# Weight preparation for the second half's stages, moved from the setup into the second to fourth samples of lane 0

## What is computed

```python
x = x + tanh(g_xattn[i]) * xattn_i(layernorm(x), ctx)
x = x + tanh(g_ffn[i])   * ffn_i(layernorm(x))          # i = 0..3
# ffn_0: two linear maps with quantised inputs and weights, depthwise convolution and silu between them
# ffn_1: a router picks one of 8 experts for each token
# ffn_2: rmsnorm, causal self attention, rmsnorm, gated silu map of width 1024 (up, down)
# ffn_3: three blocks of quantised linear maps with low-rank parts, layernorm and gelu
```

## Time and profile before

| | us |
|---|---|
| median of the runs | 2938.9 (2935.18 to 2942.4) |
| the profiled execution | 2956.94 |
| its span (first to last instruction) | 2955.7 |
| PE busy in it | 2666.5 (90%) |
| PE's weight loads | 2164.5 (73%) |
| DVE busy | 2224.2 (75%) |
| ACT busy | 1743.2 (59%) |
| POOL busy | 980.4 (33%) |
| granted TensorE clock, mean | 0.967 of full |

### The profile page before, as it was taken

The page is one execution under the profiler, slowest core; times in us unless marked ns, Lnnn a source line. Parts: engine busy times, 40 slices in busy tenths (PEclk is TensorE's granted clock), DMA queues, the critical chain, the costliest instruction groups (busy, mean ns, idle before and its releaser), DMA issues.

```text
span 2955.7 us, 61780 instructions
## 1 busy us (share of the span) xinstructions
PE 2666.5 (90%) x24164; PEld 2164.5 (73%) x24164; DVE 2224.2 (75%) x5402; ACT 1743.2 (59%) x4657; POOL 980.4 (33%) x1404
## 2 busy tenths in 40 slices
PE   6888999898899989898899999899999998997988
PEld 4767777677677767677677777778777877776766
DVE  7677686868676776867677777778877886867888
ACT  4667667676566666676465555556565655653433
POOL 2222313222433433223533442333322333224545
PEclk8899999999999999999999999999999999998999
DMA  5000000000011211100011221000000001001010
GB/s 179 5 21 11 21 10 19 10 14 17 19 46 51 69 46 37 31 12 26 19 39 57 62 73 35 24 23 17 21 17 16 20 18 30 5 5 33 29 40 19
DMA packets 84091, 92.20 MB, mean 31 GB/s; under 512 B 15252, under 2 KB 77208, under 8 KB 83800
## 3 DMA queue, kind: packets, MB, share of 16 engines
q1 hardware_dynamic: 75352, 59.91, 6.5%
q0 software_dynamic: 8448, 28.34, 3.3%
HBM read 65.36 MB, written 22.85 MB: 30 GB/s over the span
## 4 chain that ended last, share of the span: by engine, by line
PE 53%; DVE 32%; ACT 6%; issue 4%; POOL 3%; DMA 1%; another core or an unknown queue 1%; SPq 0%; DVEq 0%; POOLq 0%; ACTq 0%
PE psum L387 12%; PE psum L363 11%; PE psum L356 9%; PE psum L413 5%; DVE tiny L735 5%; DVE big L743 4%; PE psum L425 3%; PE psum L542 3%; PE psum L380 2%; PE psum L370 2%; PE psum L377 2%; DVE big L822 2%; PE psum L536 2%; DVE xn L716 1%; DVE psum L732 1%
## 5 line engine op out<-in xcount | busy, mean ns | idle before, releaser
L387 PE MATMUL psum<-ident,big 128*128 128x128 f32 x2816 | 423.6, 286 | 75.9 <-ACT big L1221 36.3
L1399 POOL TENSOR_TENSOR tiny<-tiny,minus_half 128x1 f32<-128x1 f32 x224 | 129.7, 579 | 994.8 <-DVE tiny L706 993.9
L1221 ACT ACTIVATE big<-big 128x512 f32<-128x512 f32 x512 | 312.3, 632 | 227.8 <-DVE big L743 226.1
L387 PEld LDWEIGHTS psum<-ident,big 128*128 128x128 f32 x2816 | 324.1, 145 | 145.4 <-ACT big L1221 68.7
L735 DVE TENSOR_REDUCE tiny<-psum 128x8 f32<-128x1024 f32 x256 | 312.8, 1222 | 54.3 <-PE psum L413 49.4
L743 DVE TENSOR_TENSOR big<-psum,tiny 128x512 f32<-128x512 f32 x512 | 330.0, 686 | 8.8
L413 PE MATMUL psum<-head_keys,small 64*128 64x256 f32 x2048 | 284.1, 400 | 23.6 <-ACT big L1228 13.9
L1414 POOL TENSOR_TENSOR head_keys<-big,head_rows 128x512 f32<-128x512 f32 x256 | 265.4, 1056 | 0.0
L413 PEld LDWEIGHTS psum<-head_keys,small 64*128 64x128 f32 x2048 | 183.7, 187 | 77.0 <-issue 56.4
L1439 POOL TENSOR_TENSOR big<-big,tiny 128x512 f32<-128x512 f32 x128 | 137.1, 1073 | 307.9 <-DVE tiny L778 307.5
L1265 ACT ACTIVATE big<-psum,tiny 128x128 f32<-128x128 f32 x512 | 182.1, 384 | 40.2 <-DVE tiny L773 39.9
(11 more groups left out here) (319 smaller groups left out, 6656.3 us busy)
## 6 DMA issues: line engine op xcount, KB each, us to landing
ctxT<-in_ctxT SPq DMA_DIRECT2D x64, 128.0 KB
after_L_xattn<-x SPq DMA_DIRECT2D x64, 128.0 KB, 1.7
mixture_out<-spare SPq DMA_DIRECT2D x46, 128.0 KB
x_in<-in_x SPq DMA_DIRECT2D x32, 128.0 KB
mixture_in<-xn SPq DMA_DIRECT2D x32, 128.0 KB, 1.7
x_in<-after_L_xattn SPq DMA_DIRECT2D x32, 128.0 KB
bx_in<-after_L_xattn SPq DMA_DIRECT2D x32, 128.0 KB, 2.1
out<-bout SPq DMA_DIRECT2D x32, 128.0 KB, 1.7
```

The source lines that it names most:

```text
L387: last = pe.transpose(bank[:, k * P:(k + 1) * P], src[:, k * P:(k + 1) * P], identity)
L1221: last = act.activation(flat, flat, ACT.Exp, scale=DH ** -0.5)
```

## The change

The setup ends after the fold of L1 and the planning constants. The fold of L2, the scalings for ffn_2 and the fold of L3 become turns of lane 0, at the start of the bit stage of its second, third and fourth sample. There the folds use lane 0's own bank b, free at that point. Lane 0's first wait on PE is now for the fold of L1. The second half waits for the moved steps under new names.

```diff
 SETUP = {
-    "pe": "o_L0 mean o_L1 o_L2 o_L3",
-    "dve": "ident fold_L0 bias_L0 abs clip deq r1 r2 r3 w1 s1 s2 w2 fold_L1 bias_L1 plan "
-           "fold_L2 bias_L2 down norms fold_L3 bias_L3",
+    "pe": "o_L0 mean o_L1",
+    "dve": "ident fold_L0 bias_L0 abs clip deq r1 r2 r3 w1 s1 s2 w2 fold_L1 bias_L1 plan",
...
+LATE_AT = {(1, "bit"): "L2", (2, "bit"): "self", (3, "bit"): "L3"}
...
 def pe_lane(pe, m, t):
     if t.n == 0:
-        pe.wait_ge(*m.s.dve.at(0, "setup.bias_L3"))
+        pe.wait_ge(*m.s.dve.at(0, "setup.bias_L1"))
...
         if p == 0:
-            pe.wait_ge(*m.s.dve.at(0, "setup.norms"))
+            pe.wait_ge(*m.late.dve.at(0, "late.down"))
...
+def pe_late(pe, m, t, p, l):
+    if t.n or LATE_AT.get((p, l)) not in ("L2", "L3"):
+        return
+    of = LATE_AT[(p, l)]
+    pe.wait_ge(m.loads[of], m.loaded[of])
+    pe.wait_ge(*t.dve.at(p + FREE[l][0], FREE[l][1]))
+    pe.wait_ge(*m.late.dve.at(0, f"late.fold_{of}"))
+    pe_fold(pe, m, of, t.b).then_inc(*m.late.pe.tell(0, f"late.o_{of}"))
+    yield
...
+def dve_late(dve, m, t, p, l):
+
+    if t.n or (p, l) not in LATE_AT:
+        return
+    of, w = LATE_AT[(p, l)], m.w
+    if of == "self":
+        for name, n in (("selfq", 0), ("selfk", 0), ("selfv", 0), ("gate", 1), ("up", 1)):
+            for k in range(KD):
+                last = dve.tensor_scalar(w[name][:, k, :], w[name][:, k, :], m.norms[:, n, k:k + 1], None, ALU.mult)
+        last.then_inc(*m.late.dve.tell(0, "late.norms"))
+        yield
+        dve.tensor_scalar(w["down"][:], w["down"][:], m.gf["L2"], 0.5, ALU.mult, ALU.mult
+                          ).then_inc(*m.late.dve.tell(0, "late.down"))
+        yield
+        return
+    dve_fold(dve, m, of).then_inc(*m.late.dve.tell(0, f"late.fold_{of}"))
+    yield
+    dve.wait_ge(*m.late.pe.at(0, f"late.o_{of}"))
+    dve.tensor_copy(m.out_bias[of][:], t.b[:, 0:D]).then_inc(*m.late.dve.tell(0, f"late.bias_{of}"))
+    yield
```

`pe_bitlinear` and `dve_bitlinear` call these first. The waits of PE, POOL and DVE for the old names move to the new ones. The order strings of all engines, those of the last part too, are written anew; their beginnings on PE:

```diff
-        "1323232314121333222111332321321213123241142222111133332211222112133122133213134223012301201031200213"
+        "1213114323231211222333112123132323131232401011103303322223311333113221300302321002213023103010323001"
```

More of the change, by code:

```diff
@@ L113 @@
 }
+LATE = {"pe": "o_L2 o_L3", "dve": "fold_L2 bias_L2 norms down fold_L3 bias_L3", "act": "", "pool": ""}
 LORA = {"pe": " ".join(f"m{n}" for n in range(NL)),
@@ L548, in pe_bitlinear @@
 def pe_bitlinear(pe, m, t, p, l):
+    yield from pe_late(pe, m, t, p, l)
     yield from pe_plan(pe, m, t, p, l)
@@ L637, in pe_fold @@
             pe.matmul(bank[:, 0:D], m.bvb[:, k, :], m.w[l + "o"][:, k, :], start=k == 0, stop=False)
-    pe.matmul(bank[:, 0:D], m.ones[0:1, :], m.w[l + "bo"][:], start=l == "L1", stop=True
-              ).then_inc(*m.s.pe.tell(0, f"setup.o_{l}"))
+    return pe.matmul(bank[:, 0:D], m.ones[0:1, :], m.w[l + "bo"][:], start=l == "L1", stop=True)
 def pe_constants(pe, m):
@@ L646, in pe_constants @@
     yield
-    for l in ("L1", "L2", "L3"):
-        pe.wait_ge(m.loads[l], m.loaded[l])
-        pe_fold(pe, m, l, m.setup_bank)
-        yield
+    pe.wait_ge(m.loads["L1"], m.loaded["L1"])
+    pe.wait_ge(*m.s.dve.at(0, "setup.fold_L1"))
+    pe_fold(pe, m, "L1", m.setup_bank).then_inc(*m.s.pe.tell(0, "setup.o_L1"))
+    yield
 def pe_lora(pe, m):
@@ L795, in then @@
         dve.wait_ge(*t.dve.at(p, f"{l}.{name}"))
+    yield from dve_late(dve, m, t, p, l)
     yield from dve_plan(dve, m, t, p, l)
@@ L1033, in dve_fold @@
             last = dve.tensor_copy(m.bvb[:, k, :], w[l + "bv"][:, k:k + 1].to_broadcast([P, P]))
-    last.then_inc(*m.s.dve.tell(0, f"setup.fold_{l}"))
+    return last
 def dve_bias(dve, m, l):
@@ L1068, in dve_constants @@
         yield
-    dve_fold(dve, m, "L1")
+    dve_fold(dve, m, "L1").then_inc(*m.s.dve.tell(0, "setup.fold_L1"))
     yield
@@ L1080, in dve_constants @@
     last.then_inc(*m.s.dve.tell(0, "setup.plan"))
-    yield
-    dve_fold(dve, m, "L2")
-    yield
-    dve_bias(dve, m, "L2")
-    dve.tensor_scalar(w["down"][:], w["down"][:], m.gf["L2"], 0.5, ALU.mult, ALU.mult
-                      ).then_inc(*m.s.dve.tell(0, "setup.down"))
-    yield
-    for name, n in (("selfq", 0), ("selfk", 0), ("selfv", 0), ("gate", 1), ("up", 1)):
-        for k in range(KD):
-            last = dve.tensor_scalar(w[name][:, k, :], w[name][:, k, :], m.norms[:, n, k:k + 1], None, ALU.mult)
-    last.then_inc(*m.s.dve.tell(0, "setup.norms"))
-    yield
-    dve_fold(dve, m, "L3")
-    yield
-    dve_bias(dve, m, "L3")
     yield
@@ L1144, in vector_program @@
     dve.wait_ge(*m.s.act.at(0, "setup.tanh"))
-    dve_fold(dve, m, "L0")
+    dve_fold(dve, m, "L0").then_inc(*m.s.dve.tell(0, "setup.fold_L0"))
     dve_bias(dve, m, "L0")
@@ L1151, in vector_program @@
         dve.wait_ge(t.ystored, 16 * 2 * tiles_of(t.n))
-    dve.wait_ge(*m.s.dve.at(0, "setup.bias_L3"))
+    dve.wait_ge(*m.late.dve.at(0, "late.bias_L3"))
     dve_lora(dve, m)
@@ L1521, in pool_lane @@
         if p == 0:
-            pool.wait_ge(*m.s.dve.at(0, "setup.bias_L2"))
+            pool.wait_ge(*m.late.dve.at(0, "late.bias_L2"))
         yield from pool_cross(pool, m, t, p, "L2", t.x[:])
@@ L1731, in shared_memory @@
         keep_signals(m.s, e, Signals(sem(e + "_setup"), names))
+    m.late = Lane()
+    for e in ("pe", "dve"):
+        keep_signals(m.late, e, Signals(sem(e + "_late"), [(0, f"late.{n}") for n in LATE[e].split()]))
     groups = ("L0", "L0 ffn", "L1", "router", "L2", "L3")
```

219 lines of the change are left out of this document (110 added, 109 removed).

## The result

The kernel after the change took 2899.9 us (median of four runs, 2898.3 to 2901.0), against 2937.0 us before (the three runs of above and a fourth, 2933.1 to 2942.4). The ratio is 0.9872 [0.9856, 0.9888]: 37 us less, where the prediction said 8 less and no more than 23. The profiled execution of after took 2899.15 us, which is its median; that of before took 2956.94 us, 20 us above its own median. So the two profiles differ by 58 us, of which only 37 are in the medians, and where sizes matter they are taken from runs with the kernel before beside them.

A forecast was written before the change was run, and what follows sets the result against it. PE was taken to set the pace most of the time, DVE in stretches. Terms -11.4 + 0 + 3.5 + 2.4 + 0.6 - 3.0 summed to -7.9 us, 2931 us as a median, range 2916 to 2950.

The forecast's parts named there:

- The early start: 55.3 to 115.7 us: lane 0 starts 60.4 us sooner, moving one L0 stage into idle PE time; -11.4 us.
- the better mix behind: Behind the early stretch: lane 0's bit stage starts sooner, spreading the crowd at 160 to 180 us; -3.0 us.
- PE would be busy for over 50 us in the stretch: Sign that the forecast is right: PE busy above 50 us from 55.3 to 115.7 us.
- The folds: First half, on PE: the two moved folds return as turns where PE is near its limit; +3.5 us.
- the 7.4 us on DVE coming back: Lane 0's later bit stages: DVE has the moved work there, charged at its 0.32 chain share; +2.4 us.
- new waits: At the moved steps: PE waits for the fold on DVE, DVE for the product, 0.3 each; +0.6 us.
- The clock: PE at 75 to 95 us: lane 0's matmuls might keep the upper clock level; 0, with a bound of -4 us.
- The new order: Whole kernel: all strings written anew, PE's idle time changes by unknown amounts; 8 us either way.
- End and last part: End of the second half and last part: same pattern of turns, same work in another order; both 0.
- The lanes' own length as the limit: Rival, chance 0.15: lanes' length, not PE, limits; a quarter of lane 0's 60.4 us, -15.1, 2924 us.
- The hidden start: Rival, chance 0.15: DVE full from 60 to 95 us, lane 0 delays the other lanes; +1.4, 2940 us.
- lanes in step: Rival, chance 0.17: from the fifth sample on, lanes enter bit in pairs and PE waits for DVE; +11, 2950 us.

The follow-up runs named there:

- e1: The kernel before, with all preparation steps kept in the setup, under the order strings of the kernel after: 2918.9 us, ratio 0.9870.
- e13: The kernel after without the work of the moved steps (folds, scalings), their turns kept and memsets keeping the signals: 2899.3 us, ratio 0.9883.
- e2: The kernel before with the steps moved as in after, but the old order strings with the late turns put in: 2970.0 us, ratio 1.0045.
- e5: The kernel after, unchanged, run again beside the kernel before in later launches: 2909.6 us, ratio 0.9833.
- e4: The kernel before, with one store (lane 3's seventh L3 result) issued on SP ahead of the last two groups of ffn_3 loads: 2950.9 us, ratio 0.9971.
- e11: The kernel before, with only the order strings of the last part (ffn_3) taken from the kernel after: 2954.5 us, ratio 0.9984.
- e8: The kernel before, order unchanged, with L3's result written to and stored from xn so mix need not wait for the store: 2951.3 us, ratio 0.9970.

## Why the prediction was wrong

**The early start and the better mix behind** stood at -11.4 and -3.0, together 14.4 us; the lead at 200 us is 12.7, and after is 9.4 us faster than e1, whose lane 0 starts 16 us later and has all of the preparation ahead of it. The size came out, partly by luck, as the picture was wrong. The forecast said that PE would be busy for over 50 us in the stretch, and it was busy for 41.3, as it still stood for the three lanes' bit on DVE: only 12 matmuls more were done there. At the 10.8 matmuls a microsecond of the earlier trace rows, the 43 more by 160 us are some 4 us, and the 77 more from 160 to 180 us another 7. So most of the gain came where before had 6.1 us of PE idle time, of which 4.0 are gone; the term for the better mix had 3.0 of it. How the 12.7 us divide between the early start and the new strings of that stretch, no run shows.

**The folds and the 7.4 us on DVE coming back** stood at +3.5 and +2.4, new waits at +0.6. Measured together: 0 under the new strings (e13; the copies' waits 0.24 us each), where the ends of the bounds, 0, were right for all three, and 11 to 13 us under the old ones (e2). The share of DVE in the chain, 0.32, is a mean over the kernel and was a bad price for work put into a single place: what such work costs hangs on the order around it.

**The clock** stood at 0, with a bound of -4 for 85 to 95 us. From 75 to 85 us it stayed at the lower level (0.50). From 85 to 95 us its mean rose to 0.67 in after and stayed at 0.50 in e5, whose lead at 200 us is within 1 us of that of after (13.4); so it was worth nothing that shows, as the sum had it.

**The step that failed is "The new order"**, with "End and last part", set at 0. The prediction knew that all strings were new. It took their effect as noise of 8 us either way, from the spread of two neighbouring stretches in the first half, and put it into the range and not into the sum. It was the larger part of the result, and had a sign. The prediction also said that no DMA is moved; but SP's string is new as well, and where it issues its loads and stores turned out to matter: one store ahead of the loads is worth 8 us in e4. With e5 and e11, which ran on two chips where before takes 2960.0 and 2960.1 us, the 50.5 us come apart so:

```
by 1300 us (12.7 by 200 us, rest of the first half 4)       16.9
1300 us to the first low-rank matmul  44.1 - 16.9           27.2
last part (2960.1 - 2954.5)                                  5.6
sum 49.7, measured 2960.0 - 2909.6                          50.5
```

44.1 is the distance of the first low-rank matmuls of e11 and e5. Nothing in the second half is touched by the move itself; there the change is in the strings alone. The prediction looked at the second half for what the moved steps do to it, found nothing due, and said "at 0". The rows that would have told were in its reach: the waits of before list 26.9 us of DVE waiting for stores at mix, and SP's string, read against them, shows 15 loads ahead of one store. Reading where lanes wait in the old second half, and whether the new strings mend that, would have given 8 of the 27 us a place and a sign.

The rivals fare no better. The lanes' own length as the limit (2924) would make the early start worth 15.1 us; it measured 9.4 to 12.7. In e1 lane 0 starts 43 us early, a quarter of which is 11 us; e1 gained 40 and was behind at 300 us, which that rival can't give. The hidden start and lanes in step have the wrong sign. The Trainium skill (Perfetto Trace Analysis, Identifying the Most-Contended Engine) takes weight-load busy time for a measure of PE; by that rule the sum was -7.7, and the same term was missing in it.

**What stays open.** Of the 27 us in the second half the store behind the loads is 8. The other 19 are not assigned; the waits show many small gaps. In before PE stood for ACT's exp (L1221) 31 times for 27.8 us from 1300 to 2600 us, in after (L1242) 34 times for 20.5; the wait for the heads' keys (L1228) is 13.3 us, with a longest of 5.5, against 7.7 and 1.1. Which turns of the strings make this, no run here has shown. The change itself was timed twice: it gave 37 us in the first launches and 50 in those of e5, where before was 23 us slower and after 10. Why is open too.

## What to carry to other kernels

Where the order of work is written out by hand and written anew with a change, the new order is a part of the change, and often the larger one: read the old order's waits over the whole kernel, not only where work moved, and ask which of them the new one mends. A long wait in a list costs if work of others is behind it and the engine has no slack there (8.3 us cost 8); short ones next to it can sum to 19 us and cost nothing. The same moved steps cost 0 under one order and 11 to 13 us under the other. An order is a whole: half of one joined to half of another lost some 27 to 62 us at the seam, so test it by what comes well behind the seam.

## What the runs showed of the hardware

DVE's normalisation of a tile (L716), 0.41 us in the middle of its 192 instances, once took 3.83 us. In before, DVE:

```profile
1886.89 3.83 DVE L716 TENSOR_SCALAR xn<-x,mv,tiny 128x256 f32<-128x256 f32 x1 [1.02 <-POOL tiny L1399]
```

and POOL beside it:

```profile
1886.81 1.05 POOL L1414 TENSOR_TENSOR head_keys<-big,head_rows 128x512 f32<-128x512 f32 x1
1887.79 0.13 POOL L1412 MEMSET small<- 128x16 f32 x1
1887.85 2.03 POOL L1414 TENSOR_TENSOR head_keys<-big,head_rows 128x512 f32<-128x512 f32 x2
1889.85 0.71 POOL L1426 TENSOR_TENSOR x<-x,out_bias_L 128x256 f32<-128x256 f32 x1
```

It began 0.08 us after the first of four tensor operations that POOL ran without a pause, and ended 0.16 us after the last (a memset of 0.13 us lies among them). The Trainium skill (SBUF — State Buffer, "SBUF: two separate sides") says that DVE, in an operation of a 2-port mode or with two SBUF inputs, and GpSimd share a pair of ports as an exclusive lock, and that the loser blocks while the other's instruction lasts. Whether L716 is such an operation the trace doesn't tell; its times agree with the page, and they would mean that the wait can go on over four instructions in a row. It is no accident of one run: in e8, from the later launches, the longest is 3.828 us again. In after, whose order is another, it is 2.18 us. It was not tried by itself, so the cause is read from the trace and not tested.
